# A 5x5 depthwise convolution: squares of pixels by images become the stationary operand, and a matrix of taps the moving one

## The chip, the cores and the metric

The kernel runs on one core of one Trainium2 chip. The metric is the device time of one execution in microseconds; three timed runs of each kernel are compared by their median.

## The reference

The input `x` is (128, 55, 55, 96) in fp32: 128 images of 55x55 pixels with 96 channels. Each channel has a 5x5 filter of its own, and the output is the input plus its filtered version, with zeros outside the image:

```python
def _L0_conv_ref(x, kernel):
    ch = x.shape[-1]
    k = jnp.transpose(kernel, (1, 2, 0))[:, :, None, :]
    y = lax.conv_general_dilated(x, k, window_strides=(1, 1), padding='SAME',
        dimension_numbers=('NHWC', 'HWIO', 'NHWC'), feature_group_count=ch)
    return x + y
```

No channel mixes with another, so both kernels go channel by channel. The `x +` is put into the taps: 1 is added to the centre tap.

## The kernel before

**Precision.** TensorE multiplies here in fp32r, a rounded form of fp32. So both kernels split the data, x = x_high + x_low, and the taps likewise, and sum three products: high taps by x_low, low taps by x_high, high taps by x_high.

**Tiling.** The host cuts a channel's plane into two strips of rows and lays pixels on partitions: a block of 4 image columns by 32 rows is 128 partitions. One such block for all 128 images is 128 columns of `x_in`, and a channel has 29 blocks, 3712 columns. The stationary operand is a 128x120 matrix of taps (`weights`), the moving operand is x: each matmul streams 512 columns (4 blocks by 128 images) and makes 120 output pixels. A block of output needs its own block and the next (`side` 0 and 1). So a PSUM bank takes 3 parts by 2 sides, 6 matmuls, and a channel takes 7 banks, 42 matmuls of 512 columns.

**Engines and their order.** All orders are written by hand, and engines meet at semaphores. SP issues every transfer from one queue: per channel one load of `x_in` (four buffers) and two stores of `y_out` (two buffers). ACT casts `x_high` (L219, two pieces) and copies finished sums out of PSUM to `y_out` (L229, three groups of banks). DVE makes `x_low` (L294, two pieces) and places the tap matrix for a channel with 8 casts (L285); every fourth channel it splits a band of taps (L266 to L273). TensorE's matmuls are L332. GpSimd works only at the start. Loops over turns of four channels are hardware loops.

Of the kernel before, what the change touches and what calls it, by code (L numbers as in the profile page):

```python
# [7 lines left out]
F32 = mybir.dt.float32  # L29
# [4 lines left out]
IMAGES, HEIGHT, WIDTH, CHANNELS = 128, 55, 55, 96  # L34
TAPS = 5
HALO = TAPS // 2
P = 128

STRIP_IN = 32
STRIP_LOAD = STRIP_IN - HALO  # L40
STRIP_OUT = STRIP_LOAD
STRIP_KEEP = STRIP_OUT - HALO
BLOCK = P // STRIP_IN
CHAIN_OUT = 2 * WIDTH + HALO
OUT_BLOCKS = CHAIN_OUT // BLOCK
IN_BLOCKS = OUT_BLOCKS + 1
OUT_PARTS = BLOCK * STRIP_OUT
KEEP_PARTS = BLOCK * STRIP_KEEP
IN_COLS = IN_BLOCKS * IMAGES
OUT_COLS = OUT_BLOCKS * IMAGES  # L50
STRIP_COLS = OUT_COLS // 2
assert BLOCK + 2 * HALO <= 2 * BLOCK and CHAIN_OUT % (2 * BLOCK) == 0 and 2 * STRIP_KEEP >= HEIGHT

ALL_BLOCKS = 3 * BLOCK - 1
ZERO_BLOCKS = BLOCK - 1
TAP_BLOCKS = TAPS + 1
BAND_COLS = TAP_BLOCKS * STRIP_IN
TAP_COLS = TAP_BLOCKS * STRIP_OUT  # L60
PAD = STRIP_IN - 1
FILTER_LEN = BAND_COLS + STRIP_IN
CENTRE = PAD + STRIP_IN * HALO + HALO
W_COLS = 2 * OUT_PARTS
HIGH, LOW = range(2)
PLACE_STEPS = 2 * BLOCK

BANK = 512
CHUNK = BANK
GROUPS = ((0, 2), (2, 4), (4, 7))  # L70
BANKS = GROUPS[-1][1]
assert CHUNK * BANKS == OUT_COLS

SPLIT_BANK = 4
PIECE_GROUPS = ((0, 1), (2,))
PIECE_IN = ((0, SPLIT_BANK * CHUNK + IMAGES), (SPLIT_BANK * CHUNK + IMAGES, IN_COLS))
PIECES = 2
UPPER, LOWER = range(2)
STRIPS = 2
STRIP_GROUPS = ((0, 1), (1, 2))  # L80
STRIP_FIRST = (OUT_PARTS - KEEP_PARTS, 0)

PER_TURN = 4
TURNS = CHANNELS // PER_TURN
SLOTS = 2
Y_SLOTS = 2


def wait_reuse(engine, semaphore, count):

    if not (isinstance(count, int) and count == 0):
        engine.wait_ge(semaphore, count)


def uses(turn, k, slots):

    return turn * (PER_TURN // slots) + k // slots


def build(nc, x, filters, out):  # L100


    with ExitStack() as ctx:
# [3 lines left out]
        def sems(name, count):  # L107
            return [ctx.enter_context(nc.semaphore(f"{name}{i}")) for i in range(count)]

        x_in = [sbuf(f"x_in{i}", [P, IN_COLS], F32) for i in range(PER_TURN)]  # L110
        x_high = [sbuf(f"x_high{i}", [P, IN_COLS], F32R) for i in range(SLOTS)]
        x_low = [sbuf(f"x_low{i}", [P, IN_COLS], F32R) for i in range(SLOTS)]
        y_out = [sbuf(f"y_out{i}", [OUT_PARTS, OUT_COLS], F32) for i in range(Y_SLOTS)]
        weights = [sbuf(f"weights{i}", [P, 2, W_COLS], F32R) for i in range(SLOTS)]

        band_in = sbuf("band_in", [P, BAND_COLS], F32)
        band = sbuf("band", [P, 2, ALL_BLOCKS * STRIP_OUT], F32R)
        taps_of_band = slice(ZERO_BLOCKS * STRIP_OUT, (ZERO_BLOCKS + TAP_BLOCKS) * STRIP_OUT)
        band_rest = sbuf("band_rest", [P, TAP_COLS], F32)
        residual = sbuf("residual", [P, TAP_COLS], F32)  # L120
# [3 lines left out]
        (warm_zeroed, warmed, residual_zeroed, residual_ready, band_zeroed, band_loaded, band_step,  # L124
         first_loaded) = (sems(n, 1)[0] for n in (
             "warm_zeroed", "warmed", "residual_zeroed", "residual_ready", "band_zeroed",
             "band_loaded", "band_step", "first_loaded"))
        x_loaded = sems("x_loaded", PER_TURN)
        high_ready = sems("high_ready", SLOTS)
        low_ready = sems("low_ready", SLOTS)  # L130
        weights_ready = sems("weights_ready", SLOTS)
        sums_done = [sems(f"sums_done{i}_", len(GROUPS)) for i in range(SLOTS)]
        products_done = [done[-1] for done in sums_done]
        banks_empty = sems("banks_empty", len(GROUPS))
        y_stored = [sems(f"y_stored{i}_", STRIPS) for i in range(Y_SLOTS)]


        bands = bass.AP(tensor=filters.tensor, offset=0,
                        ap=[[FILTER_LEN, CHANNELS], [1, STRIP_IN], [1, BAND_COLS]])

        def by_block(t, rows):
            return t.rearrange("k (b r) -> k b r", r=rows)

        def load_columns(engine, turn, k, start, end, loaded):
            engine.dma_start(x_in[k][:, start:end],  # L145
                             x[bass.ds(turn * PER_TURN + k, 1), :, start:end].rearrange("c p n -> (c p) n")
                             ).then_inc(loaded, 16)

        def load_x(engine, turn, k):

            if not (isinstance(turn, int) and turn == 0):
                engine.wait_ge(low_ready[k % SLOTS], PIECES * (uses(turn - 1, k, SLOTS) + 1))
            load_columns(engine, turn, k, 0, IN_COLS, x_loaded[k])
# [4 lines left out]
        def _(sp):  # L158
            def load_band(turn):

                wait_reuse(sp, band_step, 3 * turn)
                sp.dma_start(band_in[:, :], bands[bass.ds(turn * PER_TURN, PER_TURN), :, :]).then_inc(band_loaded, 16)
# [229 lines left out]
```

## Time and profile before

| | |
|---|---|
| three timed runs, median | 959.04 us (958.02 to 959.66) |
| profiled execution, first to last instruction (span) | 956.4 us |
| TensorE matmul (PE) busy | 936.2 us, 98% |
| TensorE weight load (PEld) busy | 732.0 us, 77% |
| VectorE (DVE) busy | 647.5 us, 68% |
| ScalarE (ACT) busy | 635.0 us, 66% |
| GpSimd (POOL) busy | 1.9 us |
| moved by DMA | 339.03 MB |

The page gives the profiled execution by its span; the median of the timed runs lies 2.6 us above it. PE is matmuls and PEld the loads of stationary operands, which run beside each other. Two matmuls overlap in the records, so their own durations do not add up to the busy time.

### The profile page before, as it was taken

To read this page: it belongs to the slowest core of one execution; us is meant where nothing else is said; L and a number is where in the kernel's file an instruction comes from. 1 tells how busy PE (TensorE), PEld (TensorE's weight loads), DVE (VectorE), ACT (ScalarE), POOL (GpSimd) and SP (SyncE) were. 2 spreads that over 40 slices of the span, in tenths; PEclk is the share of its full clock that TensorE was granted. 3 is DMA by queue.
4 is the path that set the end of the run, shared out by engine and by line. 5 is a ranking of instruction groups with operands and counts; after the bars stand their busy time and mean duration, and the time that the engine had idled before them with its cause. 6 is when DMAs were issued, how large, how long until landed. Compare 5 with 4: busy or idle time off the path is not lost.

```text
span 956.4 us, 12191 instructions
## 1 busy us (share of the span) xinstructions
PE 936.2 (98%) x4032; PEld 732.0 (77%) x4032; DVE 647.5 (68%) x1034; ACT 635.0 (66%) x482; POOL 1.9 (0%) x9
## 2 busy tenths in 40 slices
PE   4999999999999999999999999999999999999997
PEld 3777777777777777777777777777777777777775
DVE  6676667676676766666767767676666676676761
ACT  4666767676766667676767666676767676666764
POOL 0000000000000000000000000000000000000000
PEclk9999999999999999999999999999999999999999
DMA  9999999999999999999999999999999999999965
GB/s 362 363 361 359 366 353 372 364 364 366 351 373 366 347 371 358 355 361 362 375 364 368 360 345 384 358 352 360 360 368 360 361 375 365 362 370 352 374 223 168
DMA packets 41717, 339.03 MB, mean 354 GB/s; under 512 B 4720, under 2 KB 7792, under 8 KB 29424
## 3 DMA queue, kind: packets, MB, share of 16 engines
q1 hardware_dynamic: 41712, 338.97, 96.8%
q8 instruction: 2, 0.03, 0.0%
q14 instruction: 3, 0.02, 0.0%
HBM read 184.81 MB, written 154.14 MB: 354 GB/s over the span
## 4 chain that ended last, share of the span: by engine, by line
PE 98%; DMA 1%; DVE 1%; ACT 0%; issue 0%; SPq 0%; DVEq 0%
PE sums L332 98%; DMA band_in<-filters 1%; DVE x_low L294 0%; DVE weights L285 0%; ACT y_out L229 0%; SPq L145 0%; DVE band_rest L270 0%; DVE band L273 0%; DVE band L266 0%; DVEq L262 0%
## 5 line engine op out<-in xcount | busy, mean ns | idle before, releaser
L332 PE MATMUL sums<-x_high,weights 128*120 128x512 f32 x2688 | 733.1, 394 | 0.0
L332 PEld LDWEIGHTS sums<-x_high,weights 128*120 128x120 f32 x2688 | 488.3, 182 | 135.3
L229 ACT ACTIVATE y_out<-sums 120x1024 f32<-120x1024 f32 (+1 forms) x288 | 335.9, 1166 | 307.6 <-PE sums L332 307.1
L294 DVE TENSOR_TENSOR x_low<-x_in,x_high 128x2176 fp32r<-128x2176 f32 x192 | 393.3, 2089 | 83.4 <-ACT x_high L219 83.4
L332 PE MATMUL sums<-x_low,weights 128*120 128x512 f32 x1344 | 421.0, 394 | 13.9 <-DVE x_low L294 13.9
L285 DVE CAST weights<-band 32x240 fp32r<-32x240 f32 x768 | 230.7, 381 | 198.5 <-PE sums L332 189.4
L219 ACT ACTIVATE x_high<-x_in 128x2176 fp32r<-128x2176 f32 x192 | 336.4, 1752 | 8.3 <-DMA x_in<-x 8.3
L332 PEld LDWEIGHTS sums<-x_low,weights 128*120 128x120 f32 x1344 | 243.7, 181 | 82.3 <-issue 13.9
L266 DVE TENSOR_TENSOR band<-band_in,residual 128x180 fp32r<-128x180 f32 x24 | 8.2, 340 | 6.2 <-DMA band_in<-filters 6.2
L270 DVE TENSOR_TENSOR band_rest<-band,residual 128x180 f32<-128x180 f32 x24 | 8.3, 346 | 0.8
L273 DVE TENSOR_TENSOR band<-band_in,band_rest 128x180 fp32r<-128x180 f32 x24 | 8.3, 346 | 0.8
L246 ACT ACT_TABLE_LOAD x1 | 1.3, 1283 | 0.7 <-PEq L385 0.7
L200 POOL TENSOR_SCALAR_AFFINE_SELECT residual<-residual 32x180 f32<-32x180 f32 x4 | 1.4, 360 | 0.4 <-POOL residual L196 0.2
L306 DVE MEMSET band<- 128x660 f32 x1 | 0.6, 608 | 0.1
L304 DVE MEMSET warm<- 128x1 f32 x1 | 0.1, 59 | 0.8 <-PEq L385 0.8
L196 POOL MEMSET residual<- 128x180 f32 x1 | 0.2, 248 | 0.3 <-POOLq L385 0.3
L246 ACT ACTIVATE warm<-warm 128x1 f32<-128x1 f32 x1 | 0.2, 203 | 0.0
L385 POOL MEMSET const-float32-0.0<- 128x1 f32 x1 | 0.1, 98 | 0.2 <-issue 0.2
L385 POOL MEMSET const-float32-1.0<- 128x1 f32 x1 | 0.1, 98 | 0.0
L385 POOL MEMSET const-bfloat16-1.0<- 128x1 bf16 x1 | 0.1, 98 | 0.0
L385 POOL MEMSET const-uint8-127<- 128x1 uint8 x1 | 0.1, 98 | 0.0
## 6 DMA issues: line engine op xcount, KB each, us to landing
x_in<-x SPq DMA_DIRECT2D x95, 1856.0 KB, 13.1
y<-y_out SPq DMA_DIRECT2D x192, 784.0 KB, 8.8
band_in<-filters SPq DMA_DIRECT2D x24, 96.0 KB
x_in<-x SPq DMA_DIRECT2D x1, 1088.0 KB, 5.8
x_in<-x SPq DMA_DIRECT2D x1, 768.0 KB, 7.6
```

What stands on the lines that cost most here:

```text
L200: pool.affine_select(out=quadrant, in_=quadrant, compare_op=ALU.not_equal, fill=1.0, base=STRIP_IN - STRIP_OUT - CENTRE, pattern=[[STRIP_I ...
L219: act.activation(x_high[k % SLOTS][:, a:b], x_in[k][:, a:b], ACT.Copy).then_inc(high_ready[k % SLOTS], 1)
L229: act.activation(y_out[k % Y_SLOTS][:, a * CHUNK:b * CHUNK], psum[0:OUT_PARTS, a:b, :].rearrange("p b n -> p (b n)"), ACT.Copy).then_inc(b ...
L246: act.activation(warm[:, :], warm[:, :], ACT.Copy).then_inc(warmed, 1)
L266: dve.tensor_tensor(by_block(band[:, HIGH, taps_of_band], STRIP_OUT), taps, by_block(residual[:, :], STRIP_OUT), ALU.add).then_inc(band_st ...
L270: dve.tensor_tensor(band_rest[:, :], band[:, HIGH, taps_of_band].bitcast(F32), residual[:, :], ALU.subtract).then_inc(band_step, 1)
L273: dve.tensor_tensor(by_block(band[:, LOW, taps_of_band], STRIP_OUT), taps, by_block(band_rest[:, :], STRIP_OUT), ALU.subtract).then_inc(ba ...
L285: dve.tensor_copy(target.rearrange("k (s r c) -> k s c r", s=2, c=BLOCK), window.bitcast(F32).rearrange("k (s c r) -> k s c r", s=2, c=BLO ...
L294: dve.tensor_tensor(x_low[slot][:, a:b], x_in[k][:, a:b], x_high[slot][:, a:b].bitcast(F32), ALU.subtract).then_inc(low_ready[slot], 1)
L306: dve.memset(band[:, :, :].bitcast(F32), 0.0).then_inc(band_zeroed, 1)
L332: product = pe.matmul(psum[0:OUT_PARTS, bank, :], weights[slot][:, w, side * OUT_PARTS:(side + 1) * OUT_PARTS], v[slot][:, first:first + C ...
L385: nc = bacc.Bacc("TRN2", target_bir_lowering=False, num_devices=1)
```

## The change

The two operands of TensorE trade places. The plane is cut into 5x5 squares of 11x11 pixels. A square's 121 pixels are the partitions, and 128 images are the 128 columns of the stationary operand. What moves is a matrix in Toeplitz form made from the taps (`matrix`, 121 x 15 rows x 20 columns, in a high and a low part): a window of it, 13 or 15 rows by 14 or 16 columns, gives all output pixels that the square reaches, its own 121 and two more on each side. The result has the images as partitions and output pixels as columns.

Outputs of neighbouring squares overlap by 4 rows or columns. Inside a tile of 1 to 3 squares of one strip they add up in PSUM (one bank). Between tiles they do not: a channel has 13 tiles, ACT copies the part of each tile that is new to `y_out`, and DVE adds the seams (19 adds of 36 to 140 elements) from PSUM onto `y_out`. GpSimd now makes the tap matrices, DVE casts the first piece of `x_high`, and every loop is unrolled in the program.

| per channel | before | after |
|---|---|---|
| matmuls | 42, of 512 columns | 75, of 182, 208, 210 or 240 columns (4, 6, 6 and 9 squares, three times) |
| columns streamed | 21504 | 16188 |
| columns of a stationary operand | 120 | 128 |
| elements cast and split | 3712 | 3200 |
| PSUM to `y_out` | 3 copies, 3584 elements | 13 copies, 3025 elements |
| DVE reads of PSUM | none | 19 adds, 1344 elements |
| load | 128 rows of 14848 B | 128 rows of 12800 B |
| stores | two, of 112 rows of 7168 B | one, of 128 rows of 12160 B |

The core of the diff:

```diff
-        weights = [sbuf(f"weights{i}", [P, 2, W_COLS], F32R) for i in range(SLOTS)]
+        matrix = [sbuf(f"matrix{i}", [P, 2, MATRIX], F32R) for i in range(SLOTS)]
...
-                                product = pe.matmul(psum[0:OUT_PARTS, bank, :],
-                                                    weights[slot][:, w, side * OUT_PARTS:(side + 1) * OUT_PARTS],
-                                                    v[slot][:, first:first + CHUNK],
-                                                    start=n == 0, stop=n == len(products) - 1)
+                    wait_bank(c, t)
+                    for k in tile["squares"]:
+                        rows, cols = (tile["top"], tile["bottom"]), (even_start(k), even_end(k))
+                        target = sums(c, t, rows, cols)
+                        at = (strip * ACROSS + k) * IMAGES
+                        pe.matmul(target, x_low[c % SLOTS][0:PIXELS, at:at + IMAGES],
+                                  window(c, strip, k, slice(HIGH, HIGH + 1)).squeeze(1),
+                                  start=k == tile["squares"][0], stop=False, skip_group_check=True)
+                        for part in (LOW, HIGH):
+                            product = pe.matmul(target, x_high[c % SLOTS][0:PIXELS, at:at + IMAGES],
+                                                window(c, strip, k, slice(part, part + 1)).squeeze(1),
+                                                start=False, stop=part == HIGH and k == tile["squares"][-1],
+                                                skip_group_check=True)
+                    product.then_inc(sums_done, 1)
...
+            def add_seams(c, strip):
+                for t in strip_tiles(strip):
+                    dve.wait_ge(copied, TILE_COUNT * c + t + 1)
+                    if ADDS * c + ADDS_BEFORE[t]:
+                        dve.wait_ge(added, ADDS * c + ADDS_BEFORE[t])
+                    for rows, cols in (((tile["top"], tile["seam_rows"]), (tile["seam_cols"], tile["hi"])),
+                                       ((tile["top"], tile["bottom"]), (tile["lo"], tile["seam_cols"]))):
+                        if rows[0] < rows[1] and cols[0] < cols[1]:
+                            y = outputs(c, rows, cols)
+                            dve.tensor_tensor(y, sums(c, t, rows, cols), y, ALU.add).then_inc(added, 1)
...
+                add_seams(c, 0)
+                if following:
+                    cast_high(c + 1)
+                    split_low(c + 1, 0)
+                add_seams(c, 1)
+                if following:
+                    split_low(c + 1, 1)
+                add_seams(c, 2)
+                if following:
+                    split_low(c + 1, 2)
+                add_seams(c, 3)
+                add_seams(c, 4)
...
+            for c in range(CHANNELS):
+                if c % GROUP == 0:
+                    split_taps(c // GROUP)
+                make_matrix(c)
```

On TensorE, a stretch of the kernel before (the end of one channel: `x_low` and `x_high` move, `weights` stay, and two waits stand between banks):

```order
L332 MATMUL sums<-x_low,weights 120x512 [waits banks_empty1]
L332 MATMUL sums<-x_low,weights 120x512
L332 MATMUL sums<-x_high,weights 120x512 x4
L332 MATMUL sums<-x_low,weights 120x512 x2
L332 MATMUL sums<-x_high,weights 120x512 x4
L332 MATMUL sums<-x_low,weights 120x512 [waits banks_empty2,low_ready1]
```

and of the changed kernel, the end of channel 0 and the start of channel 1:

```order
L369 MATMUL sums<-matrix,x_low 128x15x14 [waits copied,low_ready]
L373 MATMUL sums<-matrix,x_high 128x15x14 x2
L369 MATMUL sums<-matrix,x_low 128x15x16
L373 MATMUL sums<-matrix,x_high 128x15x16 x2
L369 MATMUL sums<-matrix,x_low 128x15x16 [waits added]
L373 MATMUL sums<-matrix,x_high 128x15x16 x2
L369 MATMUL sums<-matrix,x_low 128x15x16
L373 MATMUL sums<-matrix,x_high 128x15x16 x2
L369 MATMUL sums<-matrix,x_low 128x210 [waits added]
```

Every matmul now brings its own stationary operand of 128 images, streams less than half as many columns, and nearly every tile waits for `added`, the count of DVE's seam adds, where banks waited for ACT's copies before.

On DVE, two channels of the kernel before:

```order
L285 CAST weights<-band 32x2x4x30 [waits sums_done1_2]
L285 CAST weights<-band 32x2x4x30 x7
L294 TENSOR_TENSOR x_low<-x_in,x_high 128x2176 [waits high_ready1]
L294 TENSOR_TENSOR x_low<-x_in,x_high 128x1536 [waits high_ready1]
L285 CAST weights<-band 32x2x4x30 [waits sums_done0_2]
```

and the first half of one channel of the changed kernel:

```order
L287 CAST x_high<-x_in 121x640 [waits sums_done,x_loaded2]
L296 TENSOR_TENSOR x_low<-x_in,x_high 121x640 [waits cast_done]
L313 TENSOR_TENSOR y_out<-sums,y_out 128x4x24 [waits added,copied]
L313 TENSOR_TENSOR y_out<-sums,y_out 128x4x22 [waits added,copied]
L313 TENSOR_TENSOR y_out<-sums,y_out 128x15x4
L313 TENSOR_TENSOR y_out<-sums,y_out 128x4x9 [waits added,copied]
L313 TENSOR_TENSOR y_out<-sums,y_out 128x15x4
L296 TENSOR_TENSOR x_low<-x_in,x_high 121x1280 [waits high_ready]
```

The 8 casts of weights are gone, and 19 short adds stand between the long splits of the next channel; most of them wait for DVE's own add before (`added`) and for ACT (`copied`).

## Rows read from the trace of the kernel before

**Rows 1.** The page, busy time: us, share of the span, instructions.
```profile
PE 936.2 (98%) x4032; PEld 732.0 (77%) x4032; DVE 647.5 (68%) x1034; ACT 635.0 (66%) x482; POOL 1.9 (0%) x9
```
**Rows 2.** The chain that ended last, in time order: start, us, what.
```profile
...
13.80 0.14 issue
13.94 936.22 PE sums L332 x4032
950.15 0.02 issue
950.18 1.45 ACT y_out L229
```
**Rows 3.** Who waited for whom: us in total, times, longest.
```profile
ACT y_out L229 <- PE sums L332: 307.1, 100, 3.2
DVE weights L285 <- PE sums L332: 189.4, 94, 2.7
DVE x_low L294 <- ACT x_high L219: 83.4, 96, 0.9
PE sums L332 <- DVE x_low L294: 13.9, 1, 13.9
```
**Rows 4.** TensorE by form: busy us, mean ns of one, idle before.
```profile
L332 PE MATMUL sums<-x_high,weights 128*120 128x512 f32 x2688 | 733.1, 394 | 0.0
L332 PEld LDWEIGHTS sums<-x_high,weights 128*120 128x120 f32 x2688 | 488.3, 182 | 135.3
```
**Rows 5.** Timeline of weight loads, in narrow stretches at the start and at 500 us.
```profile
13.90 0.27 PEld L332 LDWEIGHTS sums<-x_low,weights 128*120 128x120 f32 x1 [13.90 <-issue]
...
14.06 0.32 PEld L332 LDWEIGHTS sums<-x_low,weights 128*120 128x120 f32 x1
...
14.49 0.32 PEld L332 LDWEIGHTS sums<-x_high,weights 128*120 128x120 f32 x1
...
500.01 0.18 PEld L332 LDWEIGHTS sums<-x_high,weights 128*120 128x120 f32 x1
...
500.24 0.18 PEld L332 LDWEIGHTS sums<-x_high,weights 128*120 128x120 f32 x1
```
**Rows 6.** The page, DMA: queue, packets, MB, share of 16 engines.
```profile
q1 hardware_dynamic: 41712, 338.97, 96.8%
```
**Rows 7.** Windows: PE busy (count), clock, DMA share, GB/s.
```profile
8.00:20.00 12.00, 6.06 (x21) 1.00 1.02 436
...
300.00:500.00 200.00, 200.00 (x864) 1.00 0.99 363
...
915.00:950.00 35.00, 35.00 (x152) 1.00 0.54 179
```
**Rows 8.** DVE by form.
```profile
L294 DVE TENSOR_TENSOR x_low<-x_in,x_high 128x2176 fp32r<-128x2176 f32 x96 | 232.9, 2426 | 82.8 <-ACT x_high L219 82.8
L285 DVE CAST weights<-band 32x240 fp32r<-32x240 f32 x768 | 230.7, 381 | 198.5 <-PE sums L332 189.4
L294 DVE TENSOR_TENSOR x_low<-x_in,x_high 128x1536 fp32r<-128x1536 f32 x96 | 168.2, 1752 | 0.6 <-ACT x_high L219 0.6
```
**Rows 9.** ACT by form.
```profile
L229 ACT ACTIVATE y_out<-sums 120x1024 f32<-120x1024 f32 x192 | 196.3, 1023 | 6.3 <-PE sums L332 5.7 <-DMA y<-y_out 0.6
L219 ACT ACTIVATE x_high<-x_in 128x2176 fp32r<-128x2176 f32 x96 | 193.4, 2014 | 7.3 <-DMA x_in<-x 7.3
L219 ACT ACTIVATE x_high<-x_in 128x1536 fp32r<-128x1536 f32 x96 | 143.0, 1490 | 1.0 <-DMA x_in<-x 1.0
L229 ACT ACTIVATE y_out<-sums 120x1536 f32<-120x1536 f32 x96 | 139.5, 1454 | 301.3 <-PE sums L332 301.3
```
**Rows 10.** Timeline of DVE at the start.
```profile
8.13 0.35 DVE L270 TENSOR_TENSOR band_rest<-band,residual 128x180 f32<-128x180 f32 x1
...
8.52 0.35 DVE L273 TENSOR_TENSOR band<-band_in,band_rest 128x180 fp32r<-128x180 f32 x1
...
8.90 2.43 DVE L285 CAST weights<-band 32x240 fp32r<-32x240 f32 x8
...
11.36 4.09 DVE L294 TENSOR_TENSOR x_low<-x_in,x_high 128x2176 fp32r<-128x2176 f32 x2
```
**Rows 11.** GpSimd by form.
```profile
L200 POOL TENSOR_SCALAR_AFFINE_SELECT residual<-residual 32x180 f32<-32x180 f32 x4 | 1.4, 360 | 0.4 <-POOL residual L196 0.2
```

## What I predict

> **What bounds the kernel now.** I read the busy times first [rows 1]: PE is busy 98% of the span, the others have a third to spare. The chain that ended last says the same [rows 2]: from 13.94 us one unbroken piece of 936.22 us is 4032 matmuls, behind it only the last copy and its store. In the list of waits PE waited once, for 13.9 us at the start, while ACT and DVE waited for PE about once per channel [rows 3]. So a channel costs 936.22 / 96 = 9.75 us, and a matmul 936.22 / 4032 = 232 ns, of which 512 columns at 2.4 GHz are 213 ns; 19 ns are beyond the columns. The granted clock in the middle is 1.00, which is 2.4 GHz [rows 7].
>
> Then the transfers, since a faster PE would ask for more of them. In the middle the 16 DMA engines are 99% busy at 363 GB/s [rows 7]; over the span 338.97 MB in 96.8% [rows 6]. So the transfers are a second bound, right behind PE. But that share alone is not proof of a ceiling: from 8 to 20 us, when mostly loads ran, the same queue moved 436 GB/s, and in the tail, mostly stores, 179 GB/s in a share of 0.54, which would be 331 GB/s at full share [rows 7].
>
> **The change, part by part**, in us per channel; 96 channels make the time.
>
> *TensorE, columns.* 16188 columns at 2.4 GHz are 6.75 us, and 75 matmuls with 19 ns beyond the columns each add 1.43: 8.17 us, or 109 ns per matmul, if nothing but the stream counts.
>
> *TensorE, stationary operands.* Each matmul needs its own, 128 columns instead of 120, and their number grows from 4032 to 7200. Before, a load takes 182 ns [rows 4] and starts when the matmul before it starts (14.49, and every 231 ns at 500 us [rows 5]), so it hides beneath 213 ns of columns. Beneath 90 ns of columns it could not if the 182 ns were occupation. What it occupies can be bounded: at the very start, with the engine at its lower level (the matmuls there follow each other by 427 ns, 512 columns at 1.2 GHz), the second load starts 0.16 us after the first [rows 5], so a load and the hand-over to its matmul need at most 160 ns: 120 columns at 1.2 GHz are 100 ns, and 60 beyond. At 2.4 GHz with 128 columns that is 53 + 60 = 113 ns. The bounds are 109 ns (hidden wholly) and 231 ns (the whole present period is load and hand-over, 182 + 49). I take 113, since the start shows a short hand-over directly: 75 x 113 = 8.5 us, 814 us in all.
>
> The Trainium skill (TensorE: Matmul & The Clock Gate, LDWEIGHTS) gives a load as its columns over 1.2 GHz, 107 ns for 128 columns, whatever the rows; by it the sum for TensorE would be 75 x 107 = 8.0 us, or still the 8.17 of the stream. The trace does not separate the two levels enough to confirm it.
>
> *Transfers.* Loads are 128 x 12800 B = 1.638 MB, stores 128 x 12160 B = 1.556 MB, together 3.195 MB instead of 3.53 MB. At 363 GB/s [rows 7] that is 8.80 us; 845 us for 96, and 3 more for 1.26 MB of taps. Bounds: at 436 GB/s throughout 7.3 us; with loads at 436 and stores at 331, 3.76 + 4.70 = 8.5 us. I take 8.8, the rate of the same mixture.
>
> *ACT.* Slope (2014 - 1490) / 640 = 0.82 ns per element, and 0.84 for copies; fixed about 230 and 165 ns [rows 9]. Casts of 2 x 1280: 2 x 1.28 = 2.56 us. Copies of 3025 elements in 13 pieces: 2.54 + 13 x 0.165 = 4.68 us. Sum 7.2 us; if every copy pays 60 ns more for its wait, 8.0. Hidden beneath DVE.
>
> *DVE.* The slope is (2426 - 1752) / 640 = 1.05 ns per element [rows 8]. Starts of two operations where the second needs the first are 8.52 - 8.13 = 0.39 us apart for 180 elements [rows 10]: 0.196 us beyond the elements. Back to back without such a need it is about 0.05: two splits of 3712 elements took 4.09 us [rows 10], which is 3.90 + 0.14 for the end of the last + 0.05; and 8 casts in 2.43 us give (2.43 - 0.38) / 7 = 0.293 for 240 elements, 0.04 beyond. A channel now has 23 operations. Elements: 3200 split and 1344 added are 4.77 us; the cast of 640 is between 0.34 (should a cast run two elements at a time) and 0.67. Ten operations need the one directly before them (9 adds and the first split): 1.96 us. The other 13: 0.65 us. Sum 7.7 to 8.05 us. That is the lower bound, since an add reads PSUM, which no DVE row shows, and 12 of the 19 wait for two semaphores. Upper bound: all 23 pay 0.196, giving 4.77 + 0.67 + 4.51 = 9.95 us. On ACT, the nearest rows, a read from PSUM is no dearer than one from SBUF (165 against 230 ns), which speaks for the lower half; the waits, and GpSimd below, for the upper. I take the middle of 8.05 and 9.95, 9.0 us: 864 us. The removed 8 casts of weights (2.4 us) are already out of this sum.
>
> The Trainium skill (VectorE: DVE Perf Modes, The TRN2 errata) prices the fixed part of a DVE operation that reads PSUM at 120 cycles against 58 from SBUF, 65 ns more; 19 x 0.065 = 1.23 us on top of 8.05 would be 9.3 us, an estimate that lies in my range.
>
> *GpSimd.* Per channel two operations of 100 and two of 300 elements, and three of 100 per four channels. The nearest row is 360 ns for 180 elements [rows 11], 2 ns each: 950 elements are 1.9 us; at three times that, 5.7 us. It works a channel ahead of PE, hidden by 9 us. Without that cover it would cost its excess over 9 us each channel.
>
> *Start and end.* PE starts when 0.33 MB of x and the first matrix are there: at about 8 us instead of 13.94 (1.2 us of issue, 3 us of loading, then DVE's cast and split, 1.5, and GpSimd's seven operations, about 3). The end behind the last matmul stays at about 6 us: two copies, three adds, a store of 0.37 MB.
>
> *Coupling.* PE waits for `added` 8 tiles back (5.5 us), while DVE's longest split is 1.4 us, so banks cover it. A store has two channels to land, 18 us, before `y_out` is reused. SP puts load c+4 ahead of store c-1, and what that load waits for is done before DVE's last adds of c-1, so it holds nothing back.
>
> **Sum.** The slowest stream is DVE at 9.0, then DMA 8.8, PE 8.5, ACT 7.2 to 8.0. 96 x 9.0 = 864, plus about 10 until DVE's first add, plus about 5 for the last store: 879 us of span; with the 2.6 us between span and median 882 us.
>
> **The rivals.**
>
> *R1, DVE lighter, the transfers set the pace.* If DVE's adds cost what the lower sum says (8.05), DMA at 8.8 us leads: 848 + 12 = 860 us; and if it moves more than 363 GB/s, since 363 was what PE asked for, PE's 113 ns give 814 + 17 = 831. For it: 436 GB/s at the start. Against: a 99% share.
>
> *R2, DVE heavier.* 9.4 to 9.95 us per channel, 917 to 970 us; from 9.8 us on it is no gain. For it: two waits per add, and GpSimd now works beside DVE, of which the trace shows nothing. Four operations of DVE per channel that each wait for half a GpSimd operation of 0.6 us would add 1.2 us: 10.2 us, 994 us, slower. The Trainium skill (SBUF — State Buffer, Who interferes with whom) says that a DVE operation with two inputs in SBUF and a GpSimd operation that reads SBUF exclude each other for a whole instruction; no row here can show it.
>
> *R3, the stationary loads set the pace (slower).* If a load and its hand-over need all of the 231 ns of now, 7200 x 0.231 = 1663 + 17 = 1680 us; if 182 ns, 1327 us. It decides from (959 - 20) / 7200 = 130 ns per matmul on. For it: the 19 ns that a matmul of now takes beyond its columns could be the load chain showing (182 + 49), and a duration of 182 ns is twice the new 90 ns of columns. Against: the 0.16 us of the first pair. The Trainium skill (TensorE: Matmul & The Clock Gate, What overlaps and what doesn't) says that a load overlaps a running matmul only in other row groups, which would put load and stream in a row: 182 + 90 = 272 ns. The trace disagrees: 182 + 213 would be 395 ns, and the period is 232.
>
> *R4, short streams of fp32r run at a lower rate than long ones (slower).* No row has one under 512 columns. At twice the time per column 2 x 6.75 + 1.4 = 14.9 us, 1450 us.
>
> *R5, nothing changes:* the 99% DMA share would have to be a ceiling in time, not bytes; but 9% of the bytes are gone.
>
> **How the numbers follow.** Forecast, 865 to 915 us: 0.42. R1 (under 865): 0.16. R2: 0.18 for 915 to 957, 0.07 slower. R3 and R4 together 0.15. R5 0.02. The measurement can tell about 0.2%, 2 us. Faster 0.76, same 0.02, slower 0.22. The range leaves out R3 and R4 and the fast end of R1: 838 to 985 us. The likeliest case alone is 865 to 915.
>
> **What would show it.** PE: 7200 matmuls whose starts average near 120 ns, with idle time whose releaser is DVE's `added`, instead of one unbroken piece. PEld: loads following each other closer than 182 ns (right), or a matmul period at 182 or more with PE never waiting (R3). DVE busy above 90%, an add of 60 to 96 elements starting 0.26 to 0.3 us after the one before it. DMA at 350 to 365 GB/s. GpSimd under 40% busy. PE's first matmul near 8 us. Wrong would be: DVE idle for `copied` (ACT leads), DVE splits longer than 1.05 ns per element plus 0.14 (GpSimd in the way), or SP waiting for nothing while DMA is at 100% (transfers lead).

## The result

The changed kernel takes 845.9 us (median of four runs, 845.39 to 846.36) against 958.9 for the kernel before on the same chip: a ratio of 0.882, 95% interval 0.8808 to 0.8833. That is 113 us less; I had forecast 77 less, 882 us, in a range of 838 to 985. The side and the range held. Which engine sets the pace did not: it is still TensorE.

The page of the changed kernel, busy times and DMA queue, which answer to [rows 1, 6]:

```profile
PE 832.9 (99%) x7200; PEld 832.7 (99%) x7200; DVE 728.6 (86%) x2212; ACT 617.9 (73%) x1442; POOL 248.5 (29%) x460
...
q1 hardware_dynamic: 28512, 307.98, 97.3%
```

Its list of waits (engine and line, what it waited for: us in total, times, longest), against [rows 3]:

```profile
POOL matrix L228 <- PE sums L373: 559.7, 94, 6.8
ACT y_out L259 <- PE sums L373: 196.2, 389, 0.8
DVE y_out L313 <- ACT y_out L259: 16.2, 72, 0.6
PE sums L369 <- POOL matrix L228: 7.0, 1, 7.0
```

PE waits once, at the start, 7.0 us instead of 13.9. DVE waited 16 us for ACT and GpSimd 560 us for PE. The window of the middle (us, PE, PEld, DVE, ACT, POOL busy with counts, clock, DMA share, GB/s):

```profile
300.00:500.00 200.00, 200.00 (x1737) 200.00 (x1735) 175.22 (x531) 148.46 (x350) 59.09 (x110) 1.00 1.00 370
```

1737 matmuls in 200 us are 115.1 ns each and, by 75, 8.64 us per channel. The DMA share is 1.00. So PE at 99%, DMA at 100% and DVE at 86% stand side by side, and the page does not say what the next step would give. The experiments do.

How the matmuls follow each other can be read from the timeline of PE over a strip (start, length, shape; squares 1, 2, 3, then 4 of 210 columns):

```profile
400.59 0.28 PE L369 MATMUL sums<-matrix,x_low 121*128 121x240 f32 x1
400.71 0.39 PE L373 MATMUL sums<-matrix,x_high 121*128 121x240 f32 x2
400.93 0.29 PE L369 MATMUL sums<-matrix,x_low 121*128 121x240 f32 x1
401.05 0.44 PE L373 MATMUL sums<-matrix,x_high 121*128 121x240 f32 x2
401.32 0.28 PE L369 MATMUL sums<-matrix,x_low 121*128 121x240 f32 x1
401.44 0.39 PE L373 MATMUL sums<-matrix,x_high 121*128 121x240 f32 x2
401.67 0.28 PE L369 MATMUL sums<-matrix,x_low 121*128 121x210 f32 x1
```

Square 1 takes 0.34 us for its three matmuls, square 3 0.35, 113 to 117 ns each; square 2, of the same 240 columns, 0.39. A strip of 13 rows in the same view:

```profile
407.20 0.28 PE L369 MATMUL sums<-matrix,x_low 121*128 121x182 f32 x1
...
407.54 0.28 PE L369 MATMUL sums<-matrix,x_low 121*128 121x208 f32 x1
...
407.88 0.29 PE L369 MATMUL sums<-matrix,x_low 121*128 121x208 f32 x1
```

Three matmuls take 0.34 us here too, 113 ns each, with 182 or 208 columns. So, square 2 aside, the time of a matmul hardly depends on its columns between 182 and 240. That is not what a stream of columns does.

### The profile page after: what moved, and what is told of

It reads as the page before. It is cut to its first block, busy times and chain, and to the rows that moved or that the text cites. A ratio compares the mean times of both kernels' runs of the same rounds, so it can differ in the third digit from the quotient of the medians.

```text
span 843.4 us, 20670 instructions
## 1 busy us (share of the span) xinstructions
PE 832.9 (99%) x7200; PEld 832.7 (99%) x7200; DVE 728.6 (86%) x2212; ACT 617.9 (73%) x1442; POOL 248.5 (29%) x460
## 4 chain that ended last, share of the span: by engine, by line
PE 99%; POOL 0%; DMA 0%; issue 0%; ACT 0%; DVE 0%; DVEq 0%
PE sums L373 66%; PE sums L369 33%; DMA first<-consts 0%; POOL matrix L228 0%; POOL expanded L217 0%; POOL taps L207 0%; POOL spare L204 0%; POOL taps L201 0%; ACT y_out L259 0%; DVE y_out L313 0%; DVEq L92 0%
## 5 line engine op out<-in xcount | busy, mean ns | idle before, releaser
L373 PE MATMUL sums<-matrix,x_high 121*128 121x240 f32 (+3 forms) x4800 | 832.4, 282 | 0.0
L373 PEld LDWEIGHTS sums<-matrix,x_high 121*128 121x128 f32 x4800 | 738.1, 192 | 0.0
L369 PE MATMUL sums<-matrix,x_low 121*128 121x240 f32 (+3 forms) x2400 | 674.6, 281 | 7.0 <-POOL matrix L228 7.0
L259 ACT ACTIVATE y_out<-sums 128x99 f32<-128x99 f32 (+6 forms) x1248 | 416.6, 379 | 216.4 <-PE sums L373 196.2
L369 PEld LDWEIGHTS sums<-matrix,x_low 121*128 121x128 f32 x2400 | 461.0, 192 | 7.0 <-POOL matrix L228 7.0
L313 DVE TENSOR_TENSOR y_out<-sums,y_out 128x60 f32<-128x60 f32 (+6 forms) x1824 | 360.1, 228 | 101.5 <-ACT y_out L259 16.2
L296 DVE TENSOR_TENSOR x_low<-x_in,x_high 121x1280 fp32r<-121x1280 f32 (+1 forms) x288 | 366.3, 1272 | 5.3 <-ACT x_high L249 2.0
L228 POOL TENSOR_TENSOR matrix<-expanded,first 121x300 fp32r<-121x300 f32 x192 | 131.5, 706 | 559.9 <-PE sums L373 559.7
L249 ACT ACTIVATE x_high<-x_in 121x1280 fp32r<-121x1280 f32 x192 | 245.0, 1276 | 5.2 <-DMA x_in<-x 5.2
L217 POOL TENSOR_TENSOR expanded<-taps,first 121x100 f32<-121x100 f32 x192 | 85.3, 464 | 7.5
```

The lines of the kernel that those rows point to most:

```text
L217: pool.tensor_tensor(expanded[0:PIXELS, part, :].rearrange("p (d a e) -> p d a e", d=TAPS, e=TAPS), rows.unsqueeze(2).broadcast_to([PIXELS ...
L228: pool.tensor_tensor(matrix[c % SLOTS][0:PIXELS, part, :].rearrange("p (b d q) -> p b d q", d=TAPS, q=ROW), expanded[0:PIXELS, part, :].re ...
L249: act.activation(x_high[c % SLOTS][0:PIXELS, cols], x_in[c % X_SLOTS][0:PIXELS, cols], ACT.Copy).then_inc(high_ready, 1)
L259: act.activation(outputs(c, rows, cols), sums(c, t, rows, cols), ACT.Copy).then_inc(copied, 1)
L296: dve.tensor_tensor(x_low[c % SLOTS][0:PIXELS, cols], x_in[c % X_SLOTS][0:PIXELS, cols], x_high[c % SLOTS][0:PIXELS, cols].bitcast(F32), A ...
L313: dve.tensor_tensor(y, sums(c, t, rows, cols), y, ALU.add).then_inc(added, 1)
```

## The experiments

Theories at the start. **L:** a matmul has a floor near 113 ns set by its stationary operand, and square 2, whose window of the tap matrix begins at an odd element, pays more. **C:** columns and a fixed cost each. **D:** the transfers set the pace. Then, which bound stands behind PE.

### Even windows (e1)

```diff
-                left = even_start(square) - (SQUARE * square - HALO) + 1
+                left = (even_start(square) - (SQUARE * square - HALO) + 1) // 2 * 2
```

> The changed kernel with every window of the tap matrix moved left to an even column (squares of columns 0, 2 and 4 read a wrong window, so their sums are not the convolution's; same number of matmuls and columns). In the changed kernel matmuls follow each other by about 113 ns whatever their 182 to 240 columns, but those of the third square of a strip, whose window starts at an odd element and is 16 wide, by 135 ns (118 with 13 rows). Theory L (a floor per matmul set by the load of its stationary operand, plus an extra for odd windows): the 135 fall to 113, 22 ns x 2 x 3 + 5 x 4 = about 0.15 us per channel, 15 us in all: 831 us, ratio 0.866. Theory D (transfers at a share of 1.00 set the pace): 846 us stays, ratio 0.882, and PE shows waits. Rival C (columns plus a fixed cost each): the third square keeps 240 columns and its 135 ns, 846 us.

Measured: 854.9 us, ratio 0.891 (0.8897 to 0.8927). Slower than the changed kernel, which no theory had. In its trace square 2 did fall to 113 ns per matmul, but PE waited for DVE:

```profile
PEld sums L369 <- DVE y_out L313: 15.0, 58, 0.5
...
300.00:500.00 200.00, 198.88 (x1712) 194.55 (x1712) 177.14 (x525) 146.56 (x342) 85.15 (x109) 1.00 1.00 366
```

A channel takes 200 / 1712 x 75 = 8.76 us. DVE, busy 87%, has become the bound, and GpSimd is busy 85 us in 200 instead of 59. The timeline of the two engines shows why (GpSimd first, then DVE):

```profile
400.22 2.60 POOL L228 TENSOR_TENSOR matrix<-expanded,first 121x300 fp32r<-121x300 f32 x2 [5.29 <-PE sums L373]
...
400.53 1.73 DVE L296 TENSOR_TENSOR x_low<-x_in,x_high 121x1280 fp32r<-121x1280 f32 x1
```

In the changed kernel the same pair of GpSimd operations falls on seam adds:

```profile
407.51 1.35 POOL L228 TENSOR_TENSOR matrix<-expanded,first 121x300 fp32r<-121x300 f32 x2 [6.47 <-PE sums L373]
...
407.27 1.92 DVE L313 TENSOR_TENSOR y_out<-sums,y_out 128x96 f32<-128x96 f32 x7
```

There two operations of GpSimd take 1.35 us and the adds go on; beside a split (both inputs in SBUF) they take 2.60 and the split 1.73 instead of 1.48. GpSimd starts the pair when PE has finished a channel. In the changed kernel that is 1.64 us after the start of DVE's last split (405.87), here 0.31 us before it: DVE lags PE by about 2 us more, and so GpSimd's work falls onto the split. Over the whole run a split of 1280 takes 1484 ns on average in the changed kernel and 1576 here.

### Even windows, GpSimd idle (e10)

```diff
-            for c in range(CHANNELS):
+            for c in range(SLOTS):
                 if c % GROUP == 0:
                     split_taps(c // GROUP)
                 make_matrix(c)
...
-                pe.wait_ge(matrix_step, 4 * (c + 1))
+                pe.wait_ge(matrix_step, 4 * (min(c, SLOTS - 1) + 1))
```

> The run with even windows (854.9 us, DVE the bound), in which GpSimd makes the tap matrices of the first two channels only and then idles (all later channels use those). Theory G (GpSimd's reads hold up DVE's splits, one of 1280 elements took 1.72 us instead of 1.48): DVE's period falls from 8.79 to 8.55 us per channel, 8.55 x 96 + 18 = 838 us, ratio 0.874, and every split of 1280 takes 1.48 us. Rival (the 8.79 us have another cause, such as waits for ACT): 855 us stays.

Measured: 833.9 us, ratio 0.8696 (0.8682 to 0.8709), 21 us less than with GpSimd at work and 4 less than the 838 of theory G. DVE's splits of 1280, and the window:

```profile
L296 DVE TENSOR_TENSOR x_low<-x_in,x_high 121x1280 fp32r<-121x1280 f32 x192 | 285.1, 1485 | 1.8 <-ACT x_high L249 1.8
...
300.00:500.00 200.00, 199.74 (x1760) 199.40 (x1759) 176.14 (x542) 151.33 (x355) 0.00 (x0) 1.00 1.00 375
```

With GpSimd at work the mean was 1576 ns. Theory G holds: of the 0.24 us per channel between the two runs (8.76 less 8.52) the splits of 1280 make 2 x 0.09. The 8.52 us per channel (200 / 1760 x 75) are what DVE's 23 operations need undisturbed.

### Fewer columns, the same number of loads (e2)

```diff
-                            product = pe.matmul(target, x_high[...],
-                                                window(c, strip, k, slice(part, part + 1)).squeeze(1),
+                            product = pe.matmul(target[:, 0:7, :], x_high[...],
+                                                window(c, strip, k, slice(part, part + 1)).squeeze(1)[:, 0:7, :],
```

> The changed kernel in which the two products with x_high take only the first 7 rows of each window (98 or 112 columns instead of 182 to 240); the product with x_low is whole; nothing else changes, the sums lack those rows. Theory L: the matmuls with x_high still follow each other by about 110 to 113 ns, so PE stays busy and the time falls by no more than the odd windows' 15 us: about 831 us. Rival C: 112 columns are 47 ns, and with 23 ns beyond the columns each such matmul takes 70 ns; PE then needs (50 x 70 + 25 x 116) = 6.4 us per channel and would wait, with the transfers at 8.5 to 8.7 us per channel as the next bound, 825 to 850 us. So the distance of the matmuls and PE's idle time decide here, not the time.

Measured: one run, 1548.8 us, where I had expected 831, or 825 to 850. A third fewer columns made the kernel 1.8 times as slow. PE never waits:

```profile
300.00:500.00 200.00, 200.00 (x940) 200.00 (x939) 96.07 (x292) 86.79 (x189) 28.65 (x57) 1.00 0.50 194
```

200 us / 940 = 213 ns per matmul. The timeline of PE, and of the weight loads:

```profile
402.22 0.52 PE L373 MATMUL sums<-matrix,x_high 121*128 121x112 f32 x2
402.54 0.52 PE L369 MATMUL sums<-matrix,x_low 121*128 121x240 f32 x1
402.86 0.52 PE L373 MATMUL sums<-matrix,x_high 121*128 121x112 f32 x2
...
402.02 0.55 PEld L373 LDWEIGHTS sums<-matrix,x_high 121*128 121x128 f32 x2
402.45 0.33 PEld L369 LDWEIGHTS sums<-matrix,x_low 121*128 121x128 f32 x1
402.66 0.55 PEld L373 LDWEIGHTS sums<-matrix,x_high 121*128 121x128 f32 x2
```

Three matmuls take 0.64 us, although two of them have 112 columns. Their starts are uneven, but the loads are an even 213 ns apart. 213 ns are 256 cycles at 1.2 GHz. The window writes 1.00 for the clock, but the page has no row of granted clock for this run at all, so the level must be read from elsewhere. A weight load takes 0.33 us here, as at the start of the kernel before (0.32 [rows 5]), and not 0.19. And e3 (below) has short stretches with a granted clock of 0.50 on record. One of them, and two loads in it:

```profile
433.00:436.30 3.30, 3.30 (x18) 3.30 (x16) 2.75 (x11) 2.94 (x8) 0.09 (x1) 0.50 1.03 389
...
433.96 0.55 PEld L370 LDWEIGHTS sums<-matrix,x_high 121*128 121x128 f32 x2
```

There too two loads take 0.55 us, 0.33 for one and 0.21 from start to start, with windows of 182 to 240 columns. So I read e2 as having run at the lower level to its end. Why it did is not shown. Theory L's floor shows (equal distances of the loads whatever the columns), at twice the price, which L had not foreseen; C, which gave 70 ns, is out.

### Stationary operands of 64 columns (e7)

```diff
-                        pe.matmul(target, x_low[c % SLOTS][0:PIXELS, at:at + IMAGES],
+                        pe.matmul(target, x_low[c % SLOTS][0:PIXELS, at:at + IMAGES // 2],
```

(and so for x_high; PSUM and `y_out` are read and written on 64 partitions, and one seam add per channel is left of 19, as in e5 and e6 below)

> The changed kernel with one seam add per channel and stationary operands of 64 columns (only images 0 to 63; the other half of the output is zero). Theory L (the floor of a matmul is 2 array cycles per column of its stationary operand: 256 cycles are 107 ns at 2.4 GHz, and 213 ns at 1.2 GHz as in the run with seven rows): the floor falls to 53 ns, and the stream sets the distance of the matmuls: 182 columns about 76 to 95 ns, 240 columns 100 to 120 ns, so the distances now differ with the columns. Rival F (a fixed time per load whatever its columns): all stay at 110 to 113 ns.

Measured: one run, 818.6 us. PE's timeline at the end of a strip of 15 rows and the start of one of 13, then in another strip of 13:

```profile
402.05 0.27 PE L369 MATMUL sums<-matrix,x_low 121*64 121x210 f32 x1
...
402.38 0.26 PE L369 MATMUL sums<-matrix,x_low 121*64 121x182 f32 x1
...
404.19 0.26 PE L369 MATMUL sums<-matrix,x_low 121*64 121x208 f32 x1
...
404.49 0.28 PE L369 MATMUL sums<-matrix,x_low 121*64 121x208 f32 x1
...
404.83 0.27 PE L369 MATMUL sums<-matrix,x_low 121*64 121x208 f32 x1
...
405.14 0.26 PE L369 MATMUL sums<-matrix,x_low 121*64 121x182 f32 x1
```

Squares 1 and 3 take 0.30 and 0.31 us, 100 to 103 ns per matmul instead of 113; square 2 (odd window) keeps 0.34. Squares of 240 columns stay at 112. The three matmuls of 182 columns take 0.29 us (402.38 to the next square at 402.67), 97 ns each; those of 210, 0.33. So with half the stationary columns the floor is gone and the stream shows; F is out. The lengths of the loads' records say how the floor goes with the columns (e7, then the changed kernel; mean ns behind the bar):

```profile
L373 PEld LDWEIGHTS sums<-matrix,x_high 121*64 121x64 f32 x4800 | 595.8, 137 | 0.0
L373 PEld LDWEIGHTS sums<-matrix,x_high 121*128 121x128 f32 x4800 | 738.1, 192 | 0.0
```

64 columns more take 55 ns more, 0.86 ns or 2 cycles of 2.4 GHz per column; at the lower level 0.22 and 0.33 us, again 2 cycles per column. Together with 213 ns at 1.2 GHz the reading that fits is: a matmul with its own stationary operand of 128 fp32r columns takes at least 256 cycles, 2 per column, 107 ns at 2.4 GHz, and a few ns more. The floor itself was seen at 128 columns only; with 64 it lies somewhere under the 97 ns of the stream.

### Shorter matmuls in the kernel before (e12)

```diff
+                                size = CHUNK if n == 0 else CHUNK // 2
-                                product = pe.matmul(psum[0:OUT_PARTS, bank, :],
+                                product = pe.matmul(psum[0:OUT_PARTS, bank, 0:size],
-                                                    v[slot][:, first:first + CHUNK],
+                                                    v[slot][:, first:first + size],
```

> The kernel before, in which five of the six products of a bank stream 256 columns instead of 512 (the first is whole; the other halves of the sums lack those products). Loads of 120 columns, floor 240 cycles = 100 ns. At 2.4 GHz 256 columns are 107 ns. If the 19 ns that 512 columns take beyond their stream are a fixed cost per matmul, the short ones follow each other by 126 ns; if they grow with the columns, by 116; if a fixed 10 ns as the run with 64 columns shows, by 117. The transfers (3.53 MB at 414 GB/s, 8.5 us per channel) then set the time: about 830 us, so the distances are to be read, not the time. A fall of the clock to the lower level would show as 213 ns.

Measured: one run, 876.5 us.

```profile
400.04 0.64 PE L333 MATMUL sums<-x_high,weights 128*120 128x256 f32 x4
400.51 0.39 PE L333 MATMUL sums<-x_low,weights 128*120 128x512 f32 x1
```

Four in 0.47 us, 118 ns each: 11 ns beyond 256 columns, not 19. Both lengths (232 and 118) lie on 0.45 ns per column and 3 fixed. My 19 ns per matmul of whatever length was too much for short ones. The time is 46 us above the 830 that I had expected, and the window shows that the transfers did not reach 414 GB/s here:

```profile
300.00:500.00 200.00, 151.21 (x924) 134.56 (x923) 150.70 (x237) 145.88 (x112) 0.00 (x0) 0.91 1.00 389
```

PE is busy 151 of the 200 us, at a mean clock of 0.91, and over the run ACT waits 219 us for stores to land. So the kernel before, too, could move more than the 363 GB/s of its middle, but with its rows and its two buffers of `y_out` only about 389.

### What stands behind PE: two products, two products with half the stores (e3, e4)

```diff
-                        pe.matmul(target, x_low[...], window(c, strip, k, slice(HIGH, HIGH + 1)).squeeze(1), ...)
...
(e4 also)
-                sp.dma_start(out[c, :, :], y_out[c % Y_SLOTS][:, :])
+                sp.dma_start(out[c, :, 0:OUT_COLS // 2], y_out[c % Y_SLOTS][:, 0:OUT_COLS // 2])
```

> The changed kernel without the product with x_low (50 matmuls per channel instead of 75; DVE still makes x_low; the sums lack that product). PE needs 50 x 0.116 = 5.8 us per channel, so the time shows the next bound. If the transfers' 370 GB/s is a ceiling: 3.195 MB / 370 = 8.63 us per channel, 829 + 15 = 840 us, ratio 0.876, DVE waits. If DVE is next: 7.6 us busy per channel, 730 + 15 = 745 us, ratio 0.78, with more than 400 GB/s. My sum of 9.0 us per channel for DVE would have given 880 us: no gain at all.

> As the run without the product with x_low, and each channel but the last stores only the first half of its output columns (0.78 MB instead of 1.56). Transfers then need 2.42 MB per channel, 6.5 us at 370 GB/s, so DVE or ACT must be the bound. DVE at 7.6 us of busy time per channel plus its short waits: 745 to 775 us, ratio 0.78 to 0.81. By my predicted 9.0 us per channel it would be 880 us.

Measured: 841.8 us, ratio 0.8773 (0.8758 to 0.8788), and 841.4, ratio 0.877 (0.8755 to 0.8784). The first alone would have passed for the ceiling of the transfers, whose 840 us it met. The second has a quarter fewer bytes and the same time, where I had expected 745 to 775 from DVE's busy time and short waits. Window and waits of e4:

```profile
300.00:500.00 200.00, 165.64 (x1160) 147.99 (x1161) 176.59 (x536) 144.11 (x347) 85.37 (x113) 0.97 0.87 282
...
PE sums L370 <- DVE y_out L313: 131.6, 236, 1.1
```

282 GB/s, and PE waits for seam adds. A channel takes 200 / 1160 x 50 = 8.62 us: DVE's chain, at a busy share of 88%. So DVE stood 0.02 (by e4) to 0.12 us (by e10) per channel behind PE in the changed kernel. The rest of its time is no slack: it lies between an add and the one that waits for it.

### The transfers' own ceiling, and PE's own pace (e6, e5)

```diff
-    return (tile["seam_rows"] > tile["top"]) + (tile["seam_cols"] > tile["lo"])
+    return 1 * (tile["strip"] == ACROSS - 1 and tile["squares"][-1] == ACROSS - 1)
```

(one seam add per channel is left of 19; e6 with two products, e5 with even windows and all three)

> The changed kernel with one seam add per channel and without the product with x_low: PE 5.8, DVE 4.5, ACT 7 us per channel, so either ACT or the transfers are the bound. If 370 GB/s is the ceiling of the transfers: 840 us, ratio 0.877. If ACT is the bound: about 96 x 7.0 + 20 = 690 us, ratio 0.72, at 440 GB/s. I expect a ceiling of the transfers between them, near 400 GB/s: 767 + 20 = 790 us, ratio 0.82.

> The changed kernel with even windows (as in the first experiment) and only one of DVE's 19 seam adds per channel (the seams' sums are left out). DVE then needs about 4.5 us per channel and can't be the bound; GpSimd's work is as before. Theory P (in the run with even windows the matmuls were faster but DVE's chain of adds, 8.6 to 8.8 us per channel, took over): PE's 75 matmuls at about 112.5 ns are 8.45 us, 811 + 15 = 826 us, ratio 0.862. Rival D (the transfers, at a share of 1.00, allow no more than 370 GB/s): 3.195 MB / 370 = 8.63 us, 843 us, ratio 0.88, and PE shows waits for banks or x.

Measured: e6 752.5 us, ratio 0.785 (0.7836 to 0.7863), well under the 790 that I had expected; e5 827.3, ratio 0.8629 (0.8615 to 0.8643). A window of each, e6 first:

```profile
300.00:500.00 200.00, 169.13 (x1296) 156.17 (x1296) 129.44 (x130) 148.45 (x387) 108.61 (x125) 1.00 1.01 414
```

```profile
300.00:500.00 200.00, 200.00 (x1783) 200.00 (x1782) 119.26 (x120) 151.41 (x358) 87.31 (x112) 1.00 1.00 381
```

The same queue moves 414 GB/s in e6, 381 in e5, 370 in the changed kernel, all at a DMA share of 1.00. D is out: the share says that some transfer was always under way. In e6, ACT waited 160 us for stores to land, so 414 is probably near the ceiling; no other run shows more from 300 to 500 us. e5 gives PE's own pace with even windows: 112.2 ns per matmul, 8.41 us per channel, as expected.

### DVE's waits relaxed (e8)

```diff
-                    if ADDS * c + ADDS_BEFORE[t]:
+                    first_of_strip = t == strip_tiles(strip)[0]
+                    if first_of_strip and ADDS * c + ADDS_BEFORE[t]:
                         dve.wait_ge(added, ADDS * c + ADDS_BEFORE[t])
...
+                            row_add = cols[0] == tile["seam_cols"] and rows[1] == tile["seam_rows"]
+                            if not row_add and strip and not first_of_strip:
+                                dve.wait_ge(added, ADDS * c + ADDS_BEFORE[t - 1] + 1)
```

> The changed kernel, whole computation, in which a seam add of a tile no longer waits for the add directly before it, but only the column add waits for the row add of the tile before, which is two adds back. A chained add starts 0.36 us after the one before it (96 elements), an unchained one 0.17. 6 to 7 of the 9 chained starts go: DVE falls from 8.6 to about 7.4 us per channel. Theory P (PE sets the pace of the changed kernel, DVE just behind it): 843 to 846 us, ratio 0.880, PE still without waits. If DVE set the pace after all: down to 820 us or lower.

Measured: 846.3 us, ratio 0.8828 (0.8813 to 0.8843): no gain alone, as theory P has it. DVE now waits where it had worked:

```profile
DVE y_out L317 <- ACT y_out L259: 137.2, 107, 1.4
```

### New tiles, with and without relaxed waits (e9, e11)

```diff
-        for squares in ((0, 1, 2), (3, 4)) if ends else ((0, 1), (2, 3), (4,)):
+        for squares in ((0, 1, 2), (3, 4)) if ends else ((0, 1), (2,), (3, 4)):
...
-            origin = even_start(squares[0])
+            origin = start_in(squares, squares[0])
...
+def start_in(squares, c):
+    return start_of(c) - 1 if squares == (2,) else even_start(c)
```

(e9 with the waits of e8 too, e11 without)

> The whole computation. In the three middle strips the squares are put into tiles as (0, 1), (2), (3, 4) instead of (0, 1), (2, 3), (4), and the tile of square 2 begins one column earlier, so that its 16 wide window starts at an even element; and the seam adds wait as in the run with relaxed waits. The matmuls of square 2 fall from 124, 135 and 135 ns to about 113 each in three strips: 55 ns x 3 = 0.165 us per channel, 16 us. DVE needs 7.4 us and can't take over, the transfers have shown 414 GB/s and need 377. Theory P: 846 - 16 = 830 us, ratio 0.866. Rival: DVE and GpSimd in each other's way keep it at 846 or more.

> As the run before it in this list, with the new tiles but with the seam adds' waits of the changed kernel. Theory P with DVE just behind: DVE's chain needs 8.6 us per channel without GpSimd in its way and 8.8 with it (in the run with even windows), PE 8.5; so DVE takes over and the time is 845 to 855 us, ratio 0.881 to 0.892. Rival (DVE has slack as its 86% busy says): 830 us.

Measured: e9 827.0 us, ratio 0.8624 (0.8612 to 0.8636), the fastest version of the whole computation; e11 859.9 us, ratio 0.8966 (0.8954 to 0.8978). Their windows:

```profile
300.00:500.00 200.00, 200.00 (x1777) 200.00 (x1776) 165.84 (x545) 151.35 (x357) 59.15 (x111) 1.00 1.00 379
```

```profile
300.00:500.00 200.00, 199.41 (x1699) 194.67 (x1698) 177.17 (x522) 146.87 (x340) 82.57 (x107) 1.00 1.00 360
```

The same faster matmuls are worth 19 us with room on DVE and cost 14 without, as DVE, itself then held up by GpSimd (its second split of a channel took 1.84 us), takes the lead:

```profile
402.36 1.84 DVE L304 TENSOR_TENSOR x_low<-x_in,x_high 121x1280 fp32r<-121x1280 f32 x1
```

e11 missed its expected 845 to 855 by 5 us: I had counted 8.8 us per channel for a held-up DVE, and it was 200 / 1699 x 75 = 8.83.

## Why the prediction was right, and where not

**TensorE's term came out right, but partly by luck.** I took 113 ns per matmul, 8.5 us per channel, from the first two loads of the kernel before. Measured: 115.1 ns, 8.64 us. What held is that neither the stream nor the 182 ns of a load's record set the distance, but load and hand-over. My parts of it (one cycle per stationary column, 53 ns at 2.4 GHz, and 60 ns fixed) did not hold: e2, e3 and e7 fit 2 cycles per column, 107 ns, and a few ns. At 1.2 GHz my parts give 107 + 60 = 167 ns, and 213 was measured; at 2.4 GHz the two errors cancel. I had read the 60 ns from a first pair of loads, 0.16 us apart, as an upper bound for every later one. The start of the changed kernel shows that it is none:

```profile
6.99 0.29 PEld L369 LDWEIGHTS sums<-matrix,x_low 121*128 121x128 f32 x1 [6.99 <-POOL matrix L228]
7.16 0.55 PEld L373 LDWEIGHTS sums<-matrix,x_high 121*128 121x128 f32 x2
7.58 0.33 PEld L369 LDWEIGHTS sums<-matrix,x_low 121*128 121x128 f32 x1
```

The second load starts 0.17 us after the first, the following ones 0.21 us apart. The missing 2 ns are the odd windows: about 55 ns for the three matmuls of square 2 in each of three strips.

**The step that failed** is "I take the middle of 8.05 and 9.95, 9.0 us: 864 us" for DVE. Undisturbed it needs 8.52 us (e10), so PE, at 8.64, led. The time came 36 us under the forecast: 9.0 less 8.64, 96 times, is 35 us. The size can be read term by term in the changed kernel's timeline, a strip's adds of 96 and 88 elements, then, behind one of 60, one of 36 and another of 60:

```profile
404.80 0.25 DVE L313 TENSOR_TENSOR y_out<-sums,y_out 128x96 f32<-128x96 f32 x1
405.15 0.25 DVE L313 TENSOR_TENSOR y_out<-sums,y_out 128x88 f32<-128x88 f32 x1
...
405.63 0.20 DVE L313 TENSOR_TENSOR y_out<-sums,y_out 128x36 f32<-128x36 f32 x1
405.75 0.21 DVE L313 TENSOR_TENSOR y_out<-sums,y_out 128x60 f32<-128x60 f32 x1
```

An add that waits for the one before starts 0.35 to 0.36 us after it: 0.26 beyond the 96 elements, not my 0.196. One that does not wait starts about 0.12 us after the one before: 0.07 to 0.08 beyond its 36 elements, against my 0.05. Nine adds of the first kind (2.3 us), the split behind the cast (0.2) and 13 of the second (1.0), with 4.77 us of elements and a cast as if of two elements at a time (0.34), are 8.6, where e10 measured 8.52. The lower sum had the structure right; its end with the fast cast was 7.7, and taking the fixed parts from SBUF rows cost it 0.8. The middle of 8.05 and 9.95 went 0.5 past what was needed. The upper bound, all 23 operations chained, was not a price that the order of instructions allowed: in it only nine adds follow the one they wait for directly. The Trainium skill (VectorE: DVE Perf Modes, The TRN2 errata) gives a fixed 120 cycles for an operation that reads PSUM and 58 for one from SBUF, 0.065 us between them; on the chained adds the trace agrees (0.196 and 0.065 are 0.26). On the others it does not: 0.02 to 0.03 more.

**Which stream leads.** I had DVE 9.0, DMA 8.8, PE 8.5. Measured needs: PE 8.64, DVE 8.52 to 8.62, DMA 3.195 MB at 414 GB/s, 7.7, ACT below both. PE leads by 0.02 to 0.12 us. So the time fell in the range of rival R1 (DVE lighter, under 865 us), given 0.16, and not in the 865 to 915 us to which I gave 0.42. R1's order was not right either: it put the transfers first, with PE alone at 831 us. Of the signs that I had named, PE's idle time behind `added` and a DVE busy above 90% did not show: PE waited once, at the start, and DVE was busy 86%. ACT was busy 6.4 us per channel, where I had 7.2.

**Transfers.** "I take 8.8, the rate of the same mixture" mistook a demand for a ceiling, though I had written the doubt beside it: e6 moved 414 GB/s. It did not show in the time, as 8.8 lay under my 9.0 for DVE and the real need, 7.7, under PE's 8.64.

**R2** was a mechanism that exists: DVE and GpSimd hold each other up. The Trainium skill (SBUF — State Buffer, Who interferes with whom) says so of DVE operations with two inputs in SBUF beside a GpSimd operation that reads SBUF, and e1 and e10 agree: 21 us. In the changed kernel it costs the long splits nothing (1484 ns, against 1485 with GpSimd idle), because GpSimd's matrix operations happen to start beneath seam adds, which read PSUM and SBUF; that is luck: the prediction had not asked where they fall. My price of 1.2 us per channel was too high: 0.24 from e1 to e10 (8.76 against 8.52), 0.3 in e11.

**R3** was right that a load sets the distance, but 107 ns and not 182 or 231 is what it occupies. The Trainium skill (TensorE: Matmul & The Clock Gate, LDWEIGHTS) gives 107 ns for 128 columns; the trace comes near it at 2.4 GHz (112 ns from load to load in e5), and disagrees at 1.2 GHz, where the distance is 213 ns. **R4** did not occur at 182 to 240 columns; at 98 to 112 (e2) a matmul took 213 ns, nearly twice, by the clock level and not by its stream. **Start and end:** PE began at 7.0 us (I said about 8), and the end behind the last matmul took 3.5 us instead of 6. **GpSimd** was busy 29%, under the 40% named.

## What to carry to other kernels

When a change makes matmuls shorter, ask what each one's stationary operand costs: in fp32r 2 array cycles per stationary column fit what was measured here, so with 128 of them windows under some 240 columns gained nothing. Busy shares do not order the bounds: DVE at 86% had no slack because the rest lay in waits for its own results, and DMA at a share of 1.00 had 12% left; what an engine needs is seen when its neighbours' work is taken away. Two bounds within 1% of each other must be eased together: faster matmuls alone made the kernel 14 us slower, with relaxed waits on DVE 19 us faster.

## What I had not expected of the hardware

- A window of 16 elements that begins at an odd element of the tap matrix takes longer than one that begins at an even one: 135 instead of 113 ns with 15 rows (240 columns), 118 with 13. Windows of 14 elements from odd elements did not exceed the floor; with 64 stationary columns (e7), where it is gone, 210 columns from an odd element took 110 ns and 208 from an even one 97 to 103, so they seem to pay too. Whether pairs of elements or wider lines are the unit was not tried.
- With two of three matmuls cut to 98 or 112 columns (e2), TensorE ran at its lower level for the whole 1547 us, although PE waited for nothing after its start. The cause is open.
- Streams of 256 and 512 fp32r columns take 118 and 232 ns, 0.45 ns per column, where one column per cycle of 2.4 GHz would be 0.417.
- A cast on DVE from SBUF to SBUF took 490 ns for 640 elements, where a split of 640 takes 847. At 1.05 ns per element the elements alone would be 672, so it goes faster than one at a time; two at a time fit, but no second length was tried.
